# A recurrent stack on one core: step loops written out, the early layers cut into 64-step pieces, and the input projection accumulated in the gates' PSUM rows

## The chip, the cores and the metric

One core of a Trainium2 chip runs one kernel. The number that counts is the device time of one execution in microseconds (us). Five engines work side by side: TensorE (PE, matmuls; its weight loads are listed as PEld), VectorE (DVE), ScalarE (ACT), GpSimd (POOL) and SyncE (SP, which issues most DMAs). They wait for each other through semaphores. Lines such as L763 are lines of the kernel before; lines of the changed kernel are named as "line 520 after".

## The reference, cut to what matters

The input x is 2 sequences of 1024 time steps, 256 wide. Four layers are applied, each added to its input:

1. attention of every token to two keys made from a condition vector (16 heads);
2. a mixture of experts: 4 blocks of shared hidden units (`silu(x sw1) * (x sw3)`) and 8 experts of 128 units with an exact gelu, of which the best 2 per token count;
3. a linear map plus a vector made from the condition;
4. a recurrence over the 1024 steps:

```python
xz = jnp.einsum('ntd,dk->ntk', x, Wx) + b
def step(carry, xz_t):
    prev_h, prev_c = carry
    z = xz_t + prev_h @ Wh
    ai, af, ao, ag = jnp.split(z, 4, axis=1)
    i = sigmoid(ai); f = sigmoid(af); o = sigmoid(ao); g = tanh(ag)
    next_c = f * prev_c + i * g
    next_h = o * jnp.tanh(next_c)
```

Layers 1 to 3 have no dependence between tokens. Layer 4 is a chain of 1024 steps, each on 2 sequences x 256 values. All arithmetic is in float32.

## The kernel before, in words

**A step of the recurrence.** PE multiplies the last h (2 columns of weights, since there are 2 sequences) with the 1024 columns of Wh. The 64 columns that belong to one j (j = 0 to 3) go to PSUM partitions 32j and on, so four products with different j run beside each other in four column strips of the array. Three groups come out one after the other: input and forget gate together (bank 0, moving tensor of 128 columns, semaphore `z_if`), the candidate (bank 1, 64 columns, `z_c`), the output gate (bank 2, 64 columns, `z_o`). That is 24 matmuls of the program. The trace lists each float32 matmul as 2 records, so 48 at L1075. DVE transposes each group in 32x32 blocks (L763, L765, L772), so that the 256 gate values lie on 128 partitions, 4 to a partition and gate. ACT takes sigmoid, tanh and sigmoid (L507, L510, L512). DVE multiplies forget gate and old cell (L769) and makes the new cell with one scan of 8 elements (L776), ACT its tanh (L514), DVE the new h (L782), and that releases PE for the next step.

**The projected input.** x Wx + b is computed for 256 steps at a time (`gate_inputs`, L1022, L700), stored to DRAM and brought back in pieces of 4 steps to `staged`. In each step 12 further matmuls (L1065, 24 records) with columns of an identity put the step's rows into the three banks before the recurrent products are added. Each waits until its bank has been transposed (`t_if`, `t_c`, `t_o`).

**The early layers.** There are 4 chunks of 256 time steps (512 tokens). Layers 1 to 3 of chunk 0, and layer 1 and the router of all four, run ahead of the recurrence. Layers 2 and 3 of chunk m+1 run as jobs in the 256 steps of chunk m: in every step one matmul of 128x128 weights on 128 tokens (L1089), its weights copied by SP to `blocks`. At the start of a chunk SP also spreads the experts' gates over all partitions (`comb_all`, 2048 KB). After step 64 of a chunk ACT takes the exact gelu of all experts at once (L530), with a table load on either side. Between two chunks the rest of `gate_inputs` runs with no step beside it.

**Loops.** Every engine runs a device loop whose body is 8 steps, or 16 in the stage of the shared units (steps 64 to 127 of a chunk), where PE's body is twice as long.

## Time and profile before

| | |
|---|---|
| median of 3 runs | 2500.44 us (2494.17 to 2506.16) |
| span of the profiled execution (first to last instruction) | 2496.8 us |
| PE busy, share of the span | 2227.9 us, 89% |
| DVE busy | 1230.2 us, 49% |
| ACT busy | 660.5 us, 26% |
| mean granted TensorE clock | 0.973 |
| instructions fetched by DMA (queues 8 and 14) | 4.93 MB |

The only own time that the page gives for the profiled execution is its span, 2496.8 us; the median of the timed runs lies 3.6 us above it. Busy time of PE counts records that lie over each other once. A busy PE is not a PE at its peak: matmuls are pipelined, and a record of 64 columns is 0.219 us long while the next begins after a fraction of that. The idle time ahead of an instruction is printed in brackets, with what ended it; "issue" is time in which the engine waited for nothing that the trace shows.

### The profile page before, as it was taken

What the parts mean: (1) busy time and instruction counts of PE and PEld (TensorE: products, weight loads), DVE (VectorE), ACT (ScalarE), POOL (GpSimd) and SP (SyncE); (2) the same over time, 40 slices, a digit from 0 to 9 for tenths busy, and PEclk for the clock granted to TensorE, in tenths of its full rate; (3) what the DMA queues carried; (4) which work ended last, traced back from release to release, by engine and by line L of the source; (5) the groups of instructions that cost most, each with busy time, mean ns of one, the idle gap of its engine ahead of it and who ended that gap; (6) DMA issues with size and microseconds to landing.
All of it is one profiled execution on the core that took longest, in us unless ns stands there. A gap on an engine that the chain in (4) does not pass through costs nothing.

```text
span 2496.8 us, 171522 instructions
## 1 busy us (share of the span) xinstructions
PE 2227.9 (89%) x75688; PEld 1647.1 (66%) x75688; DVE 1230.2 (49%) x6361; ACT 660.5 (26%) x4183; POOL 44.5 (2%) x141
## 2 busy tenths in 40 slices
PE   8989788989989988898998988799899888888888
PEld 5477666767767766676776766677677555555555
DVE  4345454545544445454554444455455455555554
ACT  1123322222222322222222232222222222222222
POOL 0000000000000000000000000000000000000000
PEclk9999999999999999999999999899999999999999
DMA  5100000000020000000002000000000100000000
GB/s 200 57 26 11 13 14 18 13 14 12 9 80 12 11 12 15 18 12 14 12 10 80 12 11 14 13 19 13 13 11 9 43 4 4 4 8 4 4 4 7
DMA packets 41946, 53.73 MB, mean 22 GB/s; under 512 B 7584, under 2 KB 35616, under 8 KB 40608
## 3 DMA queue, kind: packets, MB, share of 16 engines
q1 hardware_dynamic: 40048, 47.23, 5.8%
q8 instruction: 288, 4.72, 0.8%
q10 hardware_dynamic: 1584, 1.57, 0.2%
q14 instruction: 26, 0.21, 0.0%
HBM read 26.83 MB, written 10.55 MB: 15 GB/s over the span
## 4 chain that ended last, share of the span: by engine, by line
PE 42%; DVE 30%; ACT 17%; issue 11%; DVEq 0%; DMA 0%; ACTq 0%; SPq 0%; POOL 0%; POOLq 0%
PE bank L1075 29%; DVE bank L763 12%; ACT if_act L507 7%; DVE bank L772 7%; ACT o_act L512 6%; DVE h_ring L782 6%; DVE if_act L769 6%; PE bank L1065 4%; ACT bank L514 4%; PE bank L1089 3%; PE bank L1022 2%; PE bank L1006 1%; PE bank L912 1%; PE bank L924 1%; ACT hidden L530 0%
## 5 line engine op out<-in xcount | busy, mean ns | idle before, releaser
L1075 PE MATMUL bank<-wh_sb,h_ring 128*2 128x128 f32 (+1 forms) x49152 | 1123.4, 239 | 125.1 <-DVE h_ring L782 56.1
L1075 PEld LDWEIGHTS bank<-wh_sb,h_ring 128*2 128x2 f32 x49152 | 906.2, 85 | 321.5 <-DVE h_ring L782 284.0
L1065 PE MATMUL bank<-staged,small_sb 128*2 128x64 f32 (+1 forms) x24576 | 707.1, 239 | 51.9 <-issue 13.2
L763 DVE STREAM_TRANSPOSE bank<-bank 128x128 f32<-128x128 f32 x1024 | 338.7, 331 | 822.0 <-PE bank L1075 821.5
L1065 PEld LDWEIGHTS bank<-staged,small_sb 128*2 128x2 f32 x24576 | 440.0, 85 | 272.3 <-DVE bank L772 76.2
L507 ACT ACTIVATE if_act<-bank 128x8 f32<-128x8 f32 x1024 | 182.2, 178 | 1485.2 <-DVE bank L763 1485.1
L782 DVE TENSOR_TENSOR h_ring<-o_act,bank 128x4 f32<-128x4 f32 x1024 | 162.0, 158 | 230.7 <-ACT bank L514 230.7
L772 DVE STREAM_TRANSPOSE bank<-bank 128x64 f32<-128x64 f32 x1024 | 263.3, 257 | 8.3 <-PE bank L1075 5.7
L765 DVE STREAM_TRANSPOSE bank<-bank 128x64 f32<-128x64 f32 x1024 | 253.1, 247 | 3.7 <-PE bank L1075 1.1
L512 ACT ACTIVATE o_act<-bank 128x4 f32<-128x4 f32 x1024 | 177.3, 173 | 275.4 <-DVE bank L772 274.3
L1089 PE MATMUL bank<-stream,blocks 128*128 x768 | 195.0, 337 | 58.1 <-issue 58.1
L769 DVE TENSOR_TENSOR if_act<-if_act,bank 128x4 f32<-128x4 f32 x1024 | 162.3, 158 | 101.6 <-ACT if_act L507 14.3
L1089 PEld LDWEIGHTS bank<-stream,blocks 128*128 128x128 f32 x768 | 119.5, 196 | 108.8 <-issue 70.4
L776 DVE TENSOR_TENSOR_SCAN bank<-bank,if_act 128x8 f32<-128x8 f32 x1024 | 184.7, 180 | 0.0
L510 ACT ACTIVATE bank<-bank 128x4 f32<-128x4 f32 x1024 | 161.8, 158 | 6.7 <-DVE bank L765 6.2
L514 ACT ACTIVATE bank<-bank 128x4 f32<-128x4 f32 x1024 | 162.2, 158 | 0.1
L1089 PE MATMUL bank<-hidden,blocks 128*128 (+1 forms) x576 | 142.4, 328 | 18.8 <-issue 18.8
L1089 PEld LDWEIGHTS bank<-hidden,blocks 128*128 128x128 f32 x576 | 86.6, 190 | 53.8 <-issue 23.3
L428 POOL TENSOR_TENSOR stream<-stream,h_ring 128x32 f32 x128 | 34.2, 267 | 2352.6 <-DVE h_ring L782 2352.6
L1022 PE MATMUL bank<-wx_sb,x 128*128 128x512 f32 x104 | 45.7, 596 | 1.0 <-DVE x L686 1.0
L1022 PEld LDWEIGHTS bank<-wx_sb,x 128*128 128x128 f32 x104 | 19.4, 190 | 25.2 <-issue 22.2
L700 DVE TENSOR_TENSOR xz_sb<-bank,bias_z_sb 128x512 f32<-128x512 f32 x26 | 18.0, 691 | 27.1 <-PE bank L1022 27.1
(99 smaller groups left out, 400.0 us busy)
## 6 DMA issues: line engine op xcount, KB each, us to landing
blocks<-moe_sb SPq DMA_DIRECT2D x170, 64.0 KB, 1.8
comb_all<-comb_scratch SPq DMA_DIRECT2D x4, 2048.0 KB, 7.8
xz_scratch<-xz_sb SPq DMA_DIRECT2D x16, 512.0 KB, 2.9
staged<-xz_scratch SPq DMA_DIRECT2D x496, 16.0 KB
moe_sb<-in_moe SPq DMA_DIRECT2D x1, 2048.0 KB, 10.3
out_y<-stream SPq DMA_DIRECT2D x8, 256.0 KB, 2.7
moe_sb<-in_moe SPq DMA_DIRECT2D x1, 1536.0 KB, 15.2
stream<-in_x ACTq DMA_DIRECT2D x3, 512.0 KB, 21.6
```

The lines of the kernel that those rows point to most:

```text
L507: nc.scalar.activation(if_act[:, par, :, :, 0], t_if_b[:, 0:2, :, 0:B], ACT.Sigmoid).then_inc(a_if, 1)
L512: nc.scalar.activation(o_act[:, par, :], t_if_b[:, 2, :, 0:B], ACT.Sigmoid).then_inc(a_o, 1)
L514: nc.scalar.activation(c_tanh[:, par, :], cell_b[:, par, :, 1], ACT.Tanh).then_inc(cell_tanh, 1)
L763: nc.vector.transpose(bank[3][:, 0:2 * HC], bank[0][:, 0:2 * HC]).then_inc(t_if, 1)
L765: nc.vector.transpose(bank[4][:, 0:HC], bank[1][:, 0:HC]).then_inc(t_c, 1)
L769: nc.vector.tensor_tensor(if_act[:, par, 0, :, 1], if_act[:, par, 1, :, 0], cell_b[:, 1 - par, :, 1], ALU.mult).then_inc(kept, 1)
L772: nc.vector.transpose(bank[3][:, 2 * HC:3 * HC], bank[2][:, 0:HC]).then_inc(t_o, 1)
L776: nc.vector.tensor_tensor_scan(cell_b[:, par, :, :].rearrange("p q k -> p (q k)"), g_pairs[:, par, :, :].rearrange("p q k -> p (q k)"), if ...
L782: nc.vector.tensor_tensor(h_ring[:, u, :, :].rearrange("p c b -> p (c b)"), o_act[:, par, :], c_tanh[:, par, :], ALU.mult).then_inc(hid, 1)
L1065: last = nc.tensor.matmul(z[32 * j:32 * j + B, 0:(g1 - g0) * HC].rearrange("p (g m) -> p g m", m=HC), ident[:, k:k + HU + 1:HU], staged_v[ ...
L1075: last = nc.tensor.matmul(z[32 * j:32 * j + B, 0:(g1 - g0) * HC].rearrange("p (g m) -> p g m", m=HC), h_ring[:, prev, c, :], wh_v[:, c, g0 ...
L1089: last = nc.tensor.matmul(bank[7][:, tile * P:(tile + 1) * P], lhs(n), rhs(n, tile), start=start and u == 0, stop=stop and n == 1, skip_gr ...
```

## The change: what it does

1. **Loops.** All 1024 steps are written out; no engine has a loop or a counted register any more.
2. **Chunks.** Layers 1 to 3 are done for 64 steps (128 tokens) at a time. Chunk 0 runs ahead of the recurrence. Chunk n+1 runs as jobs in the 64 steps of chunk n by a fixed table of step numbers: scores 0, attention 2, router 4, gates 5 to 12, units 12 to 35, down projection 37 to 48 (two matmuls a step), linear map 49 and 50. Steps 51 to 63 have no job. All weights stay in SBUF: the copies to `blocks`, the round trip of `xz_scratch`, and `comb_all` are gone. The gates of an expert are spread over the partitions by a matmul with the identity (line 642 after). Stores to the output, 18 in place of 8, are all that SP issues once the loads are out.
3. **Input in the gates' rows.** The stationary operand of a recurrent product is a window of `h_ring` with zeros ahead of the two columns of h, so that the two result rows land at row 2u of the bank, u being the step's place in a group of 8. The rows of 8 steps are filled beforehand by x Wx and the bias, in one `inject` per bank and 8 steps: 12 matmuls for the forget gate, 12 for the output gate, and 24 for the bank that holds candidate (rows 0 to 15) and input gate (rows 16 to 31). The three injections fall into different steps of the 8 (3, 5 and 7). So the stationary operand has 2 to 16 columns (18 to 32 for the input gate) in place of 2.
4. **Groups.** The order is forget gate (8 matmuls), candidate and input gate into one bank (16), output gate (8): 32 of the program a step, all with a moving tensor of 64 columns. DVE transposes three times 64 columns.
5. **Input gate through tanh.** Its weights are halved once by POOL, and sigmoid(a) = (1 + tanh(a/2))/2 is used; the factor goes into the scan, which has 12 elements in place of 8. The cell is kept doubled, and its tanh has a scale of 0.5.
6. **gelu** is computed as x(1+erf(x/sqrt 2))/2, so that ACT needs one table throughout.

```diff
-                    for z, g0, g1, made, _ in groups:
-                        for c in range(C):
-                            for j in range(J):
-                                last = nc.tensor.matmul(
-                                    z[32 * j:32 * j + B, 0:(g1 - g0) * HC].rearrange("p (g m) -> p g m", m=HC),
-                                    h_ring[:, prev, c, :], wh_v[:, c, g0:g1, j, :],
-                                    start=False, stop=(c == C - 1), skip_group_check=True)
-                        last.then_inc(made, 1)
...
+            def recur(z, g, row, prev):
+                for c in range(C):
+                    for j in range(J):
+                        last = nc.tensor.matmul(z[32 * j:32 * j + row + B, 0:HC],
+                                                h_ring[:, prev, c, WIN - B - row:WIN], wh_v[:, c, g, j, :],
+                                                start=False, stop=(c == C - 1), skip_group_check=True)
+                return last
...
+            def inject(z, g, columns, bias_of, rows, start):
...
+                for c in range(C):
+                    for j in range(J):
+                        nc.tensor.matmul(z[32 * j:32 * j + rows, 0:HC], columns(c), wx_v[:, c, g, j, :],
+                                         start=(start and c == 0), stop=False, skip_group_check=True)
+                for j in range(J):
+                    nc.tensor.matmul(z[32 * j:32 * j + rows, 0:HC], bias_of, bias_v[:, g, j, :],
+                                     start=False, stop=False, skip_group_check=True)
...
+            def step(t):
+                uf, ug, uo, prev = (t + 4) % U, t % U, (t + 2) % U, (t - 1) % U
+                pe.wait_ge(hid, t + 1)
+                recur(z_f_b, GF, uf * B, prev).then_inc(z_f, 1)
+                recur(z_gi_b, GC, ug * B, prev)
+                recur(z_gi_b, GI, 16 + ug * B, prev).then_inc(z_gi, 1)
+                recur(z_o_b, GO, uo * B, prev).then_inc(z_o, 1)
+                if uf == U - 1:
+                    inject_stream(z_f_b, GF, t, t_f)
+                if ug == U - 1:
+                    inject_gi(t)
+                if uo == U - 1:
+                    inject_stream(z_o_b, GO, t, t_o)
...
+            for t in range(T):
+                step(t)
+                if t // TC + 1 < CHUNKS:
+                    side(t // TC + 1, t % TC)
```

The two injections that wait for a transpose late in the step are the one at step 7 of 8 (`inject_gi` waits for `t_gi`) and the one at step 5 of 8 (it waits for `t_o`). A job of the same step stands behind them on PE.

What PE does in a step before, in program order (L1065: input rows; L1075: recurrent products; L1089: job; the shape is the matmul's output, partitions x columns):

```order
L1075 MATMUL bank<-wh_sb,h_ring 2x128 x8
L1075 MATMUL bank<-wh_sb,h_ring 2x64 x16
L1089 ISA
L1089 MATMUL bank<-stream,blocks 128x128
L1063 REGISTER_ALU
L1065 MATMUL bank<-staged,small_sb 2x128 x4
L1065 MATMUL bank<-staged,small_sb 2x64 x8
```

What PE does after, where step 7 of 8 ends and the next step begins (lines 593 and on of that kernel: L691 recurrent products, L700 and L703 injection, L642 and L627 jobs):

```order
L691 MATMUL bank<-wh_sb,h_ring 4x64 x8
L700 MATMUL bank<-wx_sb,padded 32x64 x8
L703 MATMUL bank<-bias_sb,small_sb 32x64 x4
L700 MATMUL bank<-wx_sb,padded 16x64 x8
L703 MATMUL bank<-bias_sb,small_sb 16x64 x4
L642 MATMUL bank<-small_sb,comb 128x128
L691 MATMUL bank<-wh_sb,h_ring 10x64 x8
L691 MATMUL bank<-wh_sb,h_ring 2x64 x8
L691 MATMUL bank<-wh_sb,h_ring 18x64 x8
L691 MATMUL bank<-wh_sb,h_ring 6x64 x8
L627 MATMUL bank<-stream,moe_sb 128x128 x2
```

The input rows have left seven steps of eight, and where they stand they are 24 matmuls in a block, with a job between them and the next step's first product.

DVE before, one step (L763 and L765 transpose, L769 product, L772 transpose, L776 scan, L782 new h):

```order
L763 STREAM_TRANSPOSE bank<-bank 128x128
L765 STREAM_TRANSPOSE bank<-bank 128x64
L769 TENSOR_TENSOR if_act<-if_act,bank 128x4
L772 STREAM_TRANSPOSE bank<-bank 128x64
L776 SCALAR_TENSOR_TENSOR bank<-bank,if_act 128x8
L782 TENSOR_TENSOR h_ring<-o_act,bank 128x4
```

DVE after, one step with a job (L520 transposes the forget gate, L522 candidate and input gate, L527 the output gate; L530 is the scan; L486 is layer 2's addition):

```order
L520 STREAM_TRANSPOSE bank<-bank 128x64
L522 STREAM_TRANSPOSE bank<-bank 128x64
L525 TENSOR_TENSOR terms<-f_act,bank 128x4
L527 STREAM_TRANSPOSE bank<-bank 128x64
L530 SCALAR_TENSOR_TENSOR bank<-terms 128x12
L532 TENSOR_TENSOR h_ring<-o_act,bank 128x2x2
L486 SCALAR_TENSOR_TENSOR stream<-bank,stream 128x2x128
```

The number of operations is the same. The first transpose is half as wide, the second now stands for two gates, the scan is longer, and jobs come behind the new h.

## Rows read from the trace of the kernel before

**Rows 1.** Timeline, one step, last chunk: start us, us, engine, line, op, [idle before].

```profile
2300.44 1.06 PE L1075 MATMUL bank<-wh_sb,h_ring 128*2 128x128 f32 x48 [0.20 <-DVE h_ring L782]
2301.13 0.33 DVE L763 STREAM_TRANSPOSE bank<-bank 128x128 f32<-128x128 f32 x1 [0.74 <-PE bank L1075]
2301.37 0.25 DVE L765 STREAM_TRANSPOSE bank<-bank 128x64 f32<-128x64 f32 x1
2301.49 0.18 ACT L507 ACTIVATE if_act<-bank 128x8 f32<-128x8 f32 x1 [1.30 <-DVE bank L763]
...
2301.70 0.16 DVE L769 TENSOR_TENSOR if_act<-if_act,bank 128x4 f32<-128x4 f32 x1
2301.78 0.26 DVE L772 STREAM_TRANSPOSE bank<-bank 128x64 f32<-128x64 f32 x1
2301.97 0.18 DVE L776 TENSOR_TENSOR_SCAN bank<-bank,if_act 128x8 f32<-128x8 f32 x1
...
2302.18 0.16 ACT L514 ACTIVATE bank<-bank 128x4 f32<-128x4 f32 x1
2302.37 0.16 DVE L782 TENSOR_TENSOR h_ring<-o_act,bank 128x4 f32<-128x4 f32 x1 [0.22 <-ACT bank L514]
...
2302.59 1.06 PE L1075 MATMUL bank<-wh_sb,h_ring 128*2 128x128 f32 x48 [0.20 <-DVE h_ring L782]
```

**Rows 2.** Windows, L782 alone: window, length, DVE busy (steps), clock, DMA share, GB/s.

```profile
119.00:716.00 597.00, 40.48 (x256) 0.97 0.06 17
716.00:731.50 15.50, 0.16 (x1) 0.89 0.48 177
...
1935.00:1947.00 12.00, 0.16 (x1) 1.00 0.53 200
1947.00:2494.00 547.00, 40.34 (x255) 1.00 0.02 4
```

**Rows 3.** Timeline: three kinds of stall, first chunk.

```profile
130.20 0.29 PE L1075 MATMUL bank<-wh_sb,h_ring 128*2 128x64 f32 x6 [2.91 <-issue]
...
261.57 3.62 ACT L530 ACTIVATE hidden<-hidden 128x4096 f32<-128x4096 f32 x1
...
266.50 0.18 ACT L507 ACTIVATE if_act<-bank 128x8 f32<-128x8 f32 x1
...
305.96 0.50 PEld L1089 LDWEIGHTS bank<-stream,blocks 128*128 128x128 f32 x2 [5.18 <-issue]
...
309.73 0.33 DVE L763 STREAM_TRANSPOSE bank<-bank 128x128 f32<-128x128 f32 x1 [7.65 <-PE bank L1075]
```

**Rows 4.** Windows, front: PE, PEld, DVE, ACT, POOL busy, clock, DMA share, GB/s.

```profile
0.00:30.00 30.00, 22.77 (x94) 15.76 (x95) 6.62 (x21) 2.33 (x4) 3.04 (x6) 0.86 0.92 344
```

**Rows 5.** Timeline, front: first and last operation of one gate computation.

```profile
28.34 0.19 DVE L628 TENSOR_TENSOR sel<-s_all,small_sb 128x32 f32<-128x32 f32 x1 [0.29 <-ACT s_all L465]
...
32.34 0.19 DVE L652 TENSOR_TENSOR comb<-comb_a,comb_b 128x32 f32<-128x32 f32 x1
```

**Rows 6.** Timeline: one 128x128 job, and sixteen projections of 512 columns.

```profile
1200.79 0.49 PE L1089 MATMUL bank<-hidden,blocks 128*128 x2
...
102.64 14.00 PE L1022 MATMUL bank<-wx_sb,x 128*128 128x512 f32 x32 [1.04 <-DVE x L686]
```

**Rows 7.** Timeline, front: runs of weight loads, 16 and 128 columns wide.

```profile
11.38 0.29 PEld L865 LDWEIGHTS bank<-small_sb,k_heads 128*16 128x16 f32 x8
...
18.53 0.97 PEld L942 LDWEIGHTS bank<-small_sb,wproj_sb 128*128 128x128 f32 x8 [0.42 <-issue]
```

**Rows 8.** Timeline, the recurrent products of a step after a stall.

```profile
1009.36 1.93 PE L1075 MATMUL bank<-wh_sb,h_ring 128*2 128x128 f32 x48
```

**Rows 9.** Windows, that stretch and the last chunk (columns of Rows 4).

```profile
1001.00:1011.20 10.20, 7.14 (x148) 5.48 (x148) 1.73 (x9) 0.75 (x5) 0.00 (x0) 0.50 0.02 4
1950.00:2450.00 500.00, 433.67 (x16792) 292.61 (x16792) 254.47 (x1402) 136.26 (x935) 7.79 (x29) 1.00 0.02 4
```

**Rows 10.** Timeline, the last DMA issue.

```profile
2493.78 0.61 SPq L352 DMA_DIRECT2D out_y<-stream  x1
```

More of the change, by code:

```diff
@@ L845, in _ @@
+            layer2(0)
+            layer3(0)
+            dve.wait_ge(cleared, 5)
+            for t in range(T):
+                step(t)
+                if t // TC + 1 < CHUNKS:
+                    side(t // TC + 1, t % TC)
         @block.tensor
         def _(pe):
+            pe.wait_ge(cell, 1)
             pe.wait_ge(small_in, 16)
@@ L867, in _, with scores @@
             last.then_inc(score_made, 1)
-            def scores(i):
-                pe.wait_ge(x_in[i], 16)
-                if i > 0:
-                    pe.wait_ge(w1_out, i * B)
-                for b in range(B):
+            def scores(n):
+                pe.wait_ge(x_in[x_part(n)], 16)
+                for c in range(C):
+                    last = nc.tensor.matmul(bank[6][0:B * HEADS, 0:NT], score_w[:, c, :], stream[:, c, tokens(n)],
+                                            start=(c == 0), stop=(c == C - 1))
+                last.then_inc(scores_made, 1)
@@ new lines, in up @@
+            def up(n, j):
+                if j == 0:
+                    pe.wait_ge(s_out, n + 1)
+                elif j >= 2:
+                    pe.wait_ge(unit_out, n * UNITS + j - 1)
+                at = 4 * j if j < MS else EXPERT_AT + 2 * (j - MS)
+                for c in range(C):
+                    last = nc.tensor.matmul(bank[UP_BANK[j % 2]][:, 0:NT], moe_sb[:, at + c, :],
+                                            stream[:, c, tokens(n)], start=(c == 0), stop=(c == C - 1))
+                last.then_inc(up_made, 1)
@@ L875, in scores, with up2 @@
+            def up2(n, j):
+                out = bank[UP_BANK[j % 2]][:, NT:2 * NT]
+                pe.wait_ge(act_out, n * UNITS + j + 1)
+                if j < MS:
                     for c in range(C):
[L876 to L877 removed]
+                        last = nc.tensor.matmul(out, moe_sb[:, 4 * j + 2 + c, :], stream[:, c, tokens(n)],
@@ new lines, in up2, with down @@
+                last.then_inc(up2_made, 1)
+            def down(n, i):
+                for k2 in range(2):
+                    c, k = divmod(2 * i + k2, UNITS)
+                    if c == 0:
+                        pe.wait_ge(unit_out, n * UNITS + max(k + 1, UNITS - 1))
+                    last = nc.tensor.matmul(bank[6][:, c * NT:(c + 1) * NT], moe_sb[:, DOWN_AT + c * UNITS + k, :],
+                                            hidden[:, k, :], start=(k == 0), stop=(k == UNITS - 1))
+                if i == UNITS - 1:
+                    last.then_inc(down_made, 1)
@@ new lines, in lin @@
+            def lin(n, c):
+                pe.wait_ge(x2_out, n + 1)
+                out = bank[7][:, c * NT:(c + 1) * NT]
+                for k in range(C):
+                    nc.tensor.matmul(out, we_sb[:, k, c * P:(c + 1) * P], stream[:, k, tokens(n)],
+                                     start=(k == 0), stop=False)
+                last = nc.tensor.matmul(out, cond_out[:, c * P:(c + 1) * P], pick, start=False, stop=True)
+                if c == C - 1:
+                    last.then_inc(lin_made, 1)
@@ L1164, in _ @@
-            with pe.Fori(0, CITERS) as k:
-                steps(k + (CHUNKS - 1) * CITERS)
+            pe.wait_ge(w_in["experts"], 16)
+            for j in range(MS, UNITS):
+                up(0, j)
+                up2(0, j)
+                if j == MS + 2:
+                    pe.wait_ge(w_in["wu"], 16)
+                    pe.wait_ge(u_out, 1)
+                    for m in range(C):
+                        last = nc.tensor.matmul(bank[0][0:B, D:2 * D], u_act[:, m, :], wu_sb[:, m, :],
+                                                start=(m == 0), stop=(m == C - 1))
+                    last.then_inc(cond_made, 1)
@@ new lines, in _ @@
+            pe.wait_ge(w_in["down"], 16)
+            for i in range(UNITS):
+                down(0, i)
+            pe.wait_ge(w_in["we"], 16)
+            pe.wait_ge(cond_done, 1)
+            for c in range(C):
+                lin(0, c)
+            pe.wait_ge(halved, 2)
+            inject_stream(z_f_b, GF, -5, None)
+            inject_stream(z_o_b, GO, -3, None)
+            inject_gi(-1)
+            pe.wait_ge(halved, 3)
+            for t in range(T):
+                step(t)
+                if t // TC + 1 < CHUNKS:
+                    side(t // TC + 1, t % TC)
```

1189 lines of the change are left out of this document (431 added, 758 removed).

## The prediction, as it was put on record

> **What bounds the kernel now.** I read the timeline of one undisturbed step first, then counted steps per stretch, then looked at the stalls and at the front.
>
> The timeline [rows 1] shows a chain that never has slack. PE starts the recurrent products at 2300.44. DVE's first transpose starts 0.69 later, ACT's sigmoid at 1.05, DVE's product at 1.26, the scan at 1.53, ACT's tanh of the cell at 1.74, the new h at 1.93, and PE starts again at 2.15. Two bounds meet at the scan. Along the first gates it could not start before the product (0.16) is done at 1.42; what holds it to 1.53 is the output gate's transpose, which starts 0.08 behind the product and lets the next DVE instruction go after 0.19.
>
> The windows that hold only the instruction of the new h [rows 2] give the rest. In the last chunk 255 steps take 547 us, 2.145 each (I use 2.144; PE's two starts in the timeline are 2.15 apart). The first chunk has 256 steps in 597 us, 48 more than 256 x 2.144 = 549; the next two chunks are alike. Between two chunks stand 15.5 (twice) and 12.0 us with a single step. So the three chunks lose 3 x 48 = 144 us inside and about 37 between, 180 together. Check, with the first products at 117.67 and the last new h at 2493.16 [rows 10]: 117.7 + 1.9 + 1023 x 2.144 (2193.3) + 180 + 3.6 of tail = 2496.5, against a span of 2496.8.
>
> The stalls [rows 3] are of three kinds. PE waits for nothing visible ("issue"): 5.18 us at 305.96, where the long loop body begins again, with DVE idle for 7.65; two more like it follow in each chunk. ACT holds up a step with the gelu of 4096 elements (3.62) and a table load on either side. And PE stands for 2.91 within the first pass through a body at 130, while 2048 KB of expert gates are spread.
>
> **The change, part by part.**
>
> *Loops, gelu batch, spreading, stage between chunks.* All that made the 180 us is gone: no branch, one ACT table, no `comb_all`, no stage without steps. Minus 180, if the written-out code arrives in time (a rival below).
>
> *Front, now 117.7 us.* Chunk 0 is 128 tokens in place of 512, and only its part of layer 1 runs ahead. The start up to the score weights stays, 11.8 us. I put layer 1 of one chunk at 6 more, the gates at 3.5 (the 14 operations take 4.2 for four times the elements, and most of that is fixed [rows 5]), 12 units at 1.4 (two jobs of 0.49 [rows 6], 0.3 of ACT and hand-overs, one behind the other), 24 down products at 0.21 to 0.43 depending on the clock, and 4 for the linear map, the padding and the injections. That is 11.8+6+3.5+16.8+8+4 = 50. The 7.9 MB up to Wh need 23 us at the 344 GB/s of the first 30 [rows 4], so they don't bind. Bounds 43 and 65. Minus 68.
>
> *A step, now 2.144.* The 48 records span 1.06, a record of 64 columns takes 0.219, and counted in units of 64 columns there are 16 rounds of four strips: (1.06-0.22)/15 = 0.056 a round. The first gates' last round begins 6 units in, 0.34; with 0.27 for a record of 128 columns that leaves 0.08 until DVE starts at 0.69 [rows 1]. After the change there are again 16 rounds: forget gate 4, candidate and input gate 8, output gate 4. So DVE can start the forget gate at 3x0.056+0.22+0.08 = 0.47, candidate+input at 11x0.056+0.30 = 0.92, the output gate at 15x0.056+0.30 = 1.14. From there, by [rows 1]: transpose 0.25, hand-over 0.03, tanh of 8 elements 0.18, hand-over 0.03, so the scan may start at 1.41. On DVE the product follows the second transpose by 0.19 (1.11), the third transpose by 0.08 (1.19), the scan by 0.19 (1.38), so now the tanh holds it, at 1.41. The scan to the cell's tanh takes 0.21 and 0.02 for four more elements, then 0.19 and 0.22: next start at 2.05. Gain 0.09 a step. The forget gate is ready at 0.93, 0.18 ahead of need; if DVE is late with it, nothing moves up to there. Halving the weights costs nothing in the steps. POOL's sum (0.3 us a group of 8) lies under PE's 0.47. All steps: 50 + 1.8 + 1023 x 2.05 (2097) + 3.6 = 2153.
>
> *Injections and jobs.* The 12 program matmuls a step leave, 48 a group of 8 steps come. They start when the bank has been transposed: for candidate+input at 1.17+0.06 = 1.23, 12 rounds of 0.056 to 1.90, for the output gate at 1.50, 6 rounds to 1.84; the forget gate's ends at 1.25. Alone each fits before 2.05. A job behind it does not: a 128x128 matmul streams 0.21 (14.0 us for 32 records of 512 columns, 0.44 each, so 0.11 a record of 128, two a matmul [rows 6]). Two matmuls after `inject_gi` end at 2.33, 0.28 late, in steps 15, 39 and 47 of a chunk; one ends 0.06 late in 23 and 31; after the output gate's, two are 0.22 late in 13, 37 and 45. Sum 3x0.28+2x0.06+3x0.22 = 1.6 a chunk, 24 us for 15 chunks. What waits behind them is the whole next step. If each change between full-array and strip products costs 0.2 more in the ten exposed places, it is 30 us more. I take 30. DVE's and ACT's jobs have at most 256 and 128 columns and lie in the 0.5 us in which DVE waits for PE; the waits on jobs of the same step are met there except in those steps. 2183.
>
> *Wider stationary operands.* No row shows strips with more than 2 columns. Runs of full loads [rows 7] show 128 columns every (0.97-0.19)/7 = 0.111 us, 0.87 ns a column. If the four strips load at the same time, 32 columns take 0.03, under a round. If they load one after another, a round of R columns needs 3.5R ns: more than 0.056 above 16 columns, that is for the input gate alone (18 to 32, mean 25: 0.087). Four rounds x 0.031 = 0.12 a step. I take the first, since with 2 columns the strips' records begin side by side, and keep 0.12 x 1023 = 127 us as the upper end. By the Trainium skill, TensorEngine Tiling (Array Packing), Key Properties, different tiles can execute their weight loads and matmuls in parallel; by that the sum would get no such term. The trace before neither confirms nor denies it for wide loads.
>
> *The clock.* It is at 1.00 (2.4 GHz) throughout the last chunk [rows 9], where PE streams 16 rounds and 8 more of input rows in 2.144: 63%. It is at 0.50 (1.2 GHz) in 1001 to 1011, after PE had stood through a stall. After the change five steps of eight without a job stream 16 rounds, 0.90 of 2.05: 44%; no stretch of before lies that low without a stall. A step at half clock: 48 records span 1.93 [rows 8], a round 0.112; the output gate then arrives at 15x0.112+0.30 = 1.98, the scan starts at 2.17, the step takes 2.81, 0.76 more. I allow some 30 such steps, 20 us (bounds 0 and 100). 2203.
>
> **Sum.** 50 + 2 + 2097 + 30 + 20 + 4 = 2203 of span, and 3.6 as the median lies over the span before: 2207 us.
>
> **The rivals.**
>
> *Serial weight loads.* As above: 2207+127 = 2334. For it: a column costs time in every run of loads. Against it: the strips' products stream beside each other. 20%.
>
> *Half clock for long stretches (the other side).* If the granted clock falls in steps without a job or injection and stays down, each step costs 0.76 more. With all steps at half: 50+1023x2.81+30 = 2960. It decides from (2500-2190)/0.76 = 410 steps at half, 40%: below that the kernel is still faster. For it: 44% streaming in place of 63%. Against it: jobs and injections fill PE to 70% and more in half the steps. The Trainium skill, TensorE: Matmul & The Clock Gate, Part 1, says that the gate's state is set by how busy PE has been recently; by that rule this change is at risk, and the trace agrees that the clock falls only after PE has idled. 7% that it costs more than the gain, 8% that it costs 100 to 300 us (2300 to 2490).
>
> *Code comes too late.* PE has 38 to 40 program matmuls a step to fetch, 37 before. Stalls of 5 us at every return to the 16-step body, if they came every 16 steps, would cost 64 x 5 = 320: 2527, slower. Against it: after each such stall the body's steps run on without an issue stall, and the one at 130 fell together with 2 MB of other traffic, which is gone. 4%.
>
> **Chances.** Forecast 61%, serial loads 20%, long half clock 8% and 7%, code 4%. The likeliest case alone spans 2150 to 2260 (front 43 to 65, step 2.03 to 2.07, jobs 24 to 60, clock 0 to 60). The range 2150 to 2350 takes in serial loads and leaves out less than 2 in 10. A measurement of this kernel can tell 0.5%, 12 us, from nothing. Faster 90% (all but the two slower cases), within 0.5% 1%, slower 9%.
>
> **What would show it.** First transposes to first transposes 2.05 in steps 51 to 63 of a chunk, with L520 starting 0.47 and L522 0.92 after PE. If L522 drifts from 0.92 to 1.1 as the rows go from 18 to 32, loads are serial; if L527 starts later than 1.2, PE is slower than I count. Steps of 2.3 at 15, 39, 47. The clock row of those stretches: anything under 1.00 there means the 20 us are too few. The first h after 52 us. Idle "issue" of PE should be near nothing. The prediction is wrong if a step's period is over 2.1 at full clock, or if the clock is below 0.9.

## The result, and the profile after

The changed kernel takes 2527.55 us (median of 4 runs, 2523.85 to 2537.98) against 2500.91 of the kernel before beside it: a ratio of 1.011, 95% interval 1.009 to 1.014. It is 1.1% slower; 2207 was forecast, and the rival with the nearest mechanism, "code comes too late", had 4%.

The page of the changed kernel (busy time, clock by slices, instruction queue, the chain that ended last):

```profile
span 2536.1 us, 173932 instructions
...
PE 1946.1 (77%) x80392; PEld 1551.4 (61%) x80392; DVE 1275.4 (50%) x6871; ACT 738.7 (29%) x4322; POOL 44.1 (2%) x154
...
PEclk9999999999899999999999999999999999989999
...
q8 instruction: 630, 10.32, 1.7%
...
PE 59%; DVE 23%; issue 10%; ACT 7%; DVEq 0%; DMA 0%; SPq 0%; POOLq 0%; POOL 0%
```

PE is busy for 282 us less than before and the time is still longer. The instruction queue moves 630 pages of 16 KB, where the kernel before moved 288 (4.72 of its 4.93 MB); queue 8 carries PE's instructions, as the kernel with PE in a loop shows below. The share of "issue" in the chain, 10%, tells nothing by itself: it was 11% before. The mean granted clock is 0.956. This execution is the slowest of the four, 10 us above their median.

The timeline of a step whose chain nothing disturbs, to set beside [rows 1] (L520, L522, L527 transposes, L340 the tanh of candidate and input gate, L530 the scan, L532 the new h):

```profile
1196.55 1.08 PE L691 MATMUL bank<-wh_sb,h_ring 128*6 128x64 f32 x64
...
1197.03 0.27 DVE L520 STREAM_TRANSPOSE bank<-bank 128x64 f32<-128x64 f32 x1
...
1197.48 0.27 DVE L522 STREAM_TRANSPOSE bank<-bank 128x64 f32<-128x64 f32 x1 [0.18 <-PE bank L691]
...
1197.65 0.15 DVE L525 TENSOR_TENSOR terms<-f_act,bank 128x4 f32<-128x4 f32 x1
1197.70 0.27 DVE L527 STREAM_TRANSPOSE bank<-bank 128x64 f32<-128x64 f32 x1
1197.78 0.18 ACT L340 ACTIVATE terms<-bank 128x8 f32<-128x8 f32 x1 [0.27 <-DVE bank L522]
...
1198.06 0.19 DVE L530 TENSOR_TENSOR_SCAN bank<-terms 128x12 f32<-128x12 f32 x1
...
1198.47 0.16 DVE L532 TENSOR_TENSOR h_ring<-o_act,bank 128x4 f32<-128x4 f32 x1 [0.22 <-ACT bank L346]
...
1198.68 0.21 PEld L691 LDWEIGHTS bank<-wh_sb,h_ring 128*8 128x8 f32 x13 [0.60 <-DVE h_ring L532]
```

The transposes start 0.48 and 0.93 after PE, as forecast (0.47, 0.92). The scan starts at 1.51, not 1.41: the tanh is done at 1197.96 and the scan begins 0.10 later. The step is 2.13 long.

Two steps further on (same timeline, PE), an injection with a job behind it, and the next step:

```profile
1200.48 0.43 PE L700 MATMUL bank<-wx_sb,padded 128*32 128x64 f32 x16 [0.23 <-DVE bank L522]
...
1200.84 0.31 PE L703 MATMUL bank<-bias_sb,small_sb 1*32 1x64 f32 x8
...
1201.09 0.42 PE L700 MATMUL bank<-wx_sb,padded 128*16 128x64 f32 x16
...
1201.43 0.30 PE L703 MATMUL bank<-bias_sb,small_sb 1*16 1x64 f32 x8
...
1201.66 0.49 PE L642 MATMUL bank<-small_sb,comb 128*128 128x128 f32 x2
...
1202.08 0.56 PE L691 MATMUL bank<-wh_sb,h_ring 128*10 128x64 f32 x25
...
1203.30 0.74 PE L691 MATMUL bank<-wh_sb,h_ring 128*2 128x64 f32 x39 [0.66 <-issue]
```

The injection takes 1.18 to the job's start in place of the 0.67 of 12 rounds; the bias matmuls, which contract over 1 row and not 128, start late behind their neighbours (tried below). And in the middle of the recurrent products, whose operands are all there, PE stands for 0.66 with nothing to wait for. The view of waits sums the idle time of this kind (us, times, longest):

```profile
PEld bank L700 <- issue: 137.9, 275, 0.8
...
PEld bank L691 <- issue: 78.3, 154, 2.0
...
PE bank L691 <- issue: 48.7, 97, 1.8
```

The two lines of L691 are the interrupted recurrent products. The line of L700 is not such a place: it comes about once an injection, and in the kernel "pair alone" below, in which no recurrent burst is interrupted, the same place still has 146.3 us in 257 times. The breaks are tied to the pages of code. In the trace, 127 times a record inside a recurrent burst starts more than 0.25 us behind the one before; 122 of these breaks end 2.2 to 2.9 us after a page's transfer on queue 8 began, a stretch into which 17% of all recurrent records fall. Between 1000 and 1500 us (the DMA view of that window) 127 pages come, one per 3.94 us:

```profile
q8 instruction: 127, 2.08, 1.7%
```

**Where the 333 us between the sum (2203) and the span (2536.1) are.** I took the starts of L532, and for each of the 64 places in a chunk the shortest step among chunks 1 to 14; this "undisturbed chunk" is 145.0 us. Ten places without job or injection in it have a median of 2.133; such a step is called quiet below, and "excess" is what steps take beyond the undisturbed chunk.

| term | forecast | measured | difference |
|---|---|---|---|
| first new h | 52 | 61.4 | +9 |
| 1023 steps | 2.05 each | 2.133 each | +85 |
| injections and jobs: (145.0 - 64 x 2.133) x 15 | 30 | 127 | +97 |
| what goes beyond the undisturbed chunk | 20 (clock) | 163 | +143 |

The last row is 79 us in some 800 steps of chunks 1 to 14 at full clock, 58 in some 95 steps that touch a stretch at half clock, and 25 in the first and last chunk.

The sum of before rested on two times that [rows 10] was to show and does not; in the timeline of the kernel before they are:

```profile
117.67 0.60 PE L1075 MATMUL bank<-wh_sb,h_ring 128*2 128x128 f32 x13 [0.26 <-DVE h_ring L749]
```

```profile
2493.16 0.16 DVE L782 TENSOR_TENSOR h_ring<-o_act,bank 128x4 f32<-128x4 f32 x1 [0.23 <-ACT bank L514]
```

### The profile page after: what moved, and what is told of

The parts are those of the page before. It is cut to its first block, busy times and chain, and to the rows that moved or that the text cites. A ratio compares the mean times of both kernels' runs of the same rounds, so it can differ in the third digit from the quotient of the medians.

```text
span 2536.1 us, 173932 instructions
## 1 busy us (share of the span) xinstructions
PE 1946.1 (77%) x80392; PEld 1551.4 (61%) x80392; DVE 1275.4 (50%) x6871; ACT 738.7 (29%) x4322; POOL 44.1 (2%) x154
## 4 chain that ended last, share of the span: by engine, by line
PE 59%; DVE 23%; issue 10%; ACT 7%; DVEq 0%; DMA 0%; SPq 0%; POOLq 0%; POOL 0%
PE bank L691 41%; DVE bank L522 9%; PE bank L700 7%; DVE bank L530 5%; DVE h_ring L532 5%; ACT bank L346 4%; PE bank L703 4%; DVE bank L527 4%; PE bank L651 2%; ACT terms L340 2%; PE bank L637 1%; PE bank L642 1%; DVE terms L525 1%; PE bank L660 1%; PE bank L627 1%
## 5 line engine op out<-in xcount | busy, mean ns | idle before, releaser
L691 PE MATMUL bank<-wh_sb,h_ring 128*10 128x64 f32 (+3 forms) x65536 | 1213.3, 226 | 472.0 <-DVE h_ring L532 418.6
L691 PEld LDWEIGHTS bank<-wh_sb,h_ring 128*10 128x10 f32 (+3 forms) x65536 | 995.5, 97 | 674.1 <-DVE h_ring L532 559.6
L520 DVE STREAM_TRANSPOSE bank<-bank 128x64 f32<-128x64 f32 x1024 | 271.9, 265 | 515.0 <-PE bank L691 507.4
L337 ACT ACTIVATE f_act<-bank 128x4 f32<-128x4 f32 x1024 | 177.9, 174 | 1200.5 <-DVE bank L520 1200.5
L522 DVE STREAM_TRANSPOSE bank<-bank 128x64 f32<-128x64 f32 x1024 | 271.8, 265 | 258.9 <-PE bank L691 248.6
L527 DVE STREAM_TRANSPOSE bank<-bank 128x64 f32<-128x64 f32 x1024 | 271.7, 265 | 37.4 <-PE bank L691 30.2
L340 ACT ACTIVATE terms<-bank 128x8 f32<-128x8 f32 x1024 | 185.5, 181 | 352.8 <-DVE bank L522 352.8
L532 DVE TENSOR_TENSOR h_ring<-o_act,bank 128x4 f32<-128x4 f32 x1024 | 163.2, 159 | 231.1 <-ACT bank L346 231.1
L530 DVE TENSOR_TENSOR_SCAN bank<-terms 128x12 f32<-128x12 f32 x1024 | 192.4, 188 | 84.1 <-ACT terms L340 2.2
L346 ACT ACTIVATE bank<-bank 128x4 f32<-128x4 f32 x1024 | 162.4, 159 | 99.9 <-DVE bank L530 2.3
L703 PE MATMUL bank<-bias_sb,small_sb 1*16 1x64 f32 (+1 forms) x4112 | 164.6, 226 | 3.7 <-issue 3.3
L700 PE MATMUL bank<-wx_sb,stream 128*16 128x64 f32 x4128 | 115.2, 227 | 65.0 <-DVE bank L527 60.9
L525 DVE TENSOR_TENSOR terms<-f_act,bank 128x4 f32<-128x4 f32 x1024 | 152.4, 149 | 0.2
L627 PE MATMUL bank<-stream,moe_sb 128*128 128x128 f32 x768 | 141.2, 306 | 3.4 <-issue 2.9
L700 PE MATMUL bank<-wx_sb,padded 128*32 128x64 f32 (+1 forms) x4096 | 113.2, 226 | 29.7 <-DVE bank L522 29.0
L700 PEld LDWEIGHTS bank<-wx_sb,stream 128*16 128x16 f32 x4128 | 75.2, 99 | 87.0 <-issue 86.7
L627 PEld LDWEIGHTS bank<-stream,moe_sb 128*128 128x128 f32 x768 | 104.1, 196 | 24.9 <-issue 4.8
L700 PEld LDWEIGHTS bank<-wx_sb,padded 128*32 128x32 f32 (+1 forms) x4096 | 71.8, 104 | 63.4 <-issue 51.2
L703 PEld LDWEIGHTS bank<-bias_sb,small_sb 1*16 1x16 f32 (+1 forms) x4112 | 71.0, 93 | 61.4 <-issue 12.6
```

The costliest lines, as they stand in the source:

```text
L340: nc.scalar.activation(gi_out.rearrange("p g (c b) -> p g c b", b=B), t_gi_b[:, :, :, ug * B:(ug + 1) * B], ACT.Tanh).then_inc(a_gi, 1)
L346: nc.scalar.activation(c_tanh, cell_c, ACT.Tanh, scale=0.5).then_inc(cell_tanh, 1)
L520: nc.vector.transpose(bank[3][:, 0:HC], z_f_b[:, 0:HC]).then_inc(t_f, 1)
L522: nc.vector.transpose(bank[4][:, 0:HC], z_gi_b[:, 0:HC]).then_inc(t_gi, 1)
L527: nc.vector.transpose(bank[3][:, HC:2 * HC], z_o_b[:, 0:HC]).then_inc(t_o, 1)
L530: nc.vector.tensor_tensor_scan(cell_all, factor, addend, 0.0, ALU.mult, ALU.add).then_inc(cell, 1)
```

## The experiments

Every kernel ran beside the kernel before on the same chip; the ratios are to that. The groups of runs used different chips; the kernel before took 2498 to 2504 us beside them.

### One mended cost at a time

Two waits stand on the scan; the one for the tanh came last.

```diff
-                dve.wait_ge(kept, t + 1)
                 dve.wait_ge(a_gi, t + 1)
+                dve.wait_ge(kept, t + 1)
```

> The changed kernel with one pair of lines exchanged: the scan waits for the tanh of candidate and input gate first and for its own product second. In the trace of the changed kernel the wait for the tanh is an instruction of its own on VectorE, and the scan starts 0.065 us behind it, where before that wait stood on the scan itself and the hand-over took 0.033. Theory A (the order of the two waits costs a hand-over): a clean step falls from 2.137 to about 2.07 us, 1023 x 0.065 = 67 us less where VectorE is the bound, some 55 in all: about 2470. Rival B (the scan is held by the third transpose, or by TensorE): no change, 2527. Rival C (TensorE's code arrives no faster than one 16 KB piece in some 3.4 us, 157 instructions a step being 0.61 of a piece, 2.09 us a step): half of the gain is given back as idle time of the kind issue, about 2500.

The bias rows, 1 partition in place of 128 (the other 127 are zeros):

```diff
-        bias_sb = sb("bias_sb", [1, G4])
+        bias_sb = sb("bias_sb", [P, G4])
...
-        ones = part("ones")[0:1, :]
+        ones = part("ones")
```

> The changed kernel with the bias held on 128 partitions (127 of them zero), so that the bias matmuls of the injections contract over 128 rows like their neighbours and no longer over one. Theory A (each change of the number of rows empties the array, 0.11 to 0.14 us each, four of them in the injection for candidate and input gate): the step behind that injection falls from 2.52 to about 2.2 us, with a job behind it from 3.16 to about 2.85, the steps with job behind the output gate's injection by 0.13; 2.8 us a chunk, about 45 in all: about 2483. Rival B (the gaps are waits for code or for the weight loads): same gaps, 2527.

The job ahead of the injections that wait for a late transpose:

```diff
                 recur(z_o_b, GO, uo * B, prev).then_inc(z_o, 1)
+                if job and ahead:
+                    side(t // TC + 1, t % TC)
                 if uf == U - 1:
...
+                if job and not ahead:
+                    side(t // TC + 1, t % TC)
```

> The changed kernel with TensorE's job of a step placed ahead of the injection in the steps where the injection waits for a late transpose (steps 5 and 7 of each 8). The same instructions in another order. Theory A (the job's 0.43 plus a change of tiling of 0.2 fit into TensorE's wait for the transpose): the ten steps of a chunk that now take 2.55 to 3.16 us fall by 0.3 to 0.6 each, 4 to 5 us a chunk, 60 to 75 in all: about 2460. Rival B (TensorE has no slack there: the job only pushes the injection back by as much): within 10 us of 2527.

One extra matmul of 256 columns in steps with neither job nor injection:

```diff
+                if quiet and U - 1 not in (uf, ug, uo):
+                    pe.wait_ge(s_out, min(t // TC + 2, CHUNKS))
+                    nc.tensor.matmul(bank[6][:, 256:512], moe_sb[:, 0, :], wh_sb[:, 0, 0:256],
+                                     start=True, stop=True)
```

> The changed kernel with one extra matmul of 128x128 weights on 256 columns, whose result nobody reads, behind the recurrent products of each step that has neither job nor injection. Four more instructions in such a step. Theory A (the granted clock falls in the quiet stretches because TensorE streams too little there): clock near 1.00 in steps 52 to 63 of each chunk and in the last chunk, mean clock over 0.98, steps there 2.14 throughout, 50 to 70 us less: about 2465. Rival B (the clock falls because TensorE stands still waiting for code): mean clock stays at 0.956, time 2527 or up to 10 us more.

| run | us | ratio, 95% | undisturbed chunk | excess at full clock | mean clock |
|---|---|---|---|---|---|
| changed kernel | 2527.55 | 1.011 (1.009 to 1.014) | 145.0 | 79 | 0.956 |
| scan's wait | 2494.98 | 0.998 (0.996 to 1.001) | 141.3 | 101 | 0.956 |
| bias on 128 rows | 2495.64 | 0.999 (0.997 to 1.002) | 141.2 | 118 | 0.965 |
| job first | 2494.46 | 0.998 (0.996 to 1.000) | 140.9 | 107 | 0.955 |
| filler | 2492.58 | 0.997 (0.995 to 1.000) | 144.8 | 103 | 0.993 |

The undisturbed chunk or the clock shows that each cost was real. With the waits exchanged the scan follows the tanh by 0.03 (timeline of that kernel):

```profile
1201.04 0.18 ACT L340 ACTIVATE terms<-bank 128x8 f32<-128x8 f32 x1 [0.27 <-DVE bank L522]
1201.25 0.19 DVE L530 TENSOR_TENSOR_SCAN bank<-terms 128x12 f32<-128x12 f32 x1
```

and the quiet step is 2.071. With 128 rows an injection's bias starts 0.22 to 0.23 behind the x rows, not 0.34 to 0.36 (timeline of PE, the same place in the group of 8):

```profile
1199.91 0.43 PE L700 MATMUL bank<-wx_sb,padded 128*32 128x64 f32 x16 [0.25 <-DVE bank L522]
1200.13 0.32 PE L703 MATMUL bank<-bias_sb,small_sb 128*32 128x64 f32 x8
1200.24 0.43 PE L700 MATMUL bank<-wx_sb,padded 128*16 128x64 f32 x16
1200.47 0.32 PE L703 MATMUL bank<-bias_sb,small_sb 128*16 128x64 f32 x8
1200.72 0.49 PE L642 MATMUL bank<-small_sb,comb 128*128 128x128 f32 x2
```

To the job's start it is 0.81, not 1.18. But all four arrive within 3 us of each other, although the undisturbed chunks promise 56 to 62 us (3.7 to 4.1 x 15) for three of them, and a clock of 0.993 about 50 for the fourth. In each the excess at full clock rises, by 22 to 39 us. That is what something else that holds the rate would do.

### Is it the code? The same instructions from a loop

> The scan's wait for the tanh alone, the bias on 128 rows and the jobs ahead of the injections, all three. Without losses their undisturbed chunks add up: 3.7 + 3.8 + 4.1 = 11.6 us shorter than the 145.0 of the changed kernel, 174 us for 15 chunks. Theory 'code arrives too slowly' (a page of 16 KB, 256 PE records' worth of instructions, cannot come more often than about every 3.4 us, and 630 pages are needed): the excess over the undisturbed chunk grows again, by 60 to 100 us, and the time is 2400 to 2450. Rival 'the three overlap in the same steps and nothing is given back': the undisturbed chunk itself falls by less than 8 us and the excess stays at 135. Second rival 'nothing is lost': 2527 - 174 = 2353.

The next two leave work out, as their expectation says. PE's instructions are the same in both but for the loop and its registers:

```diff
-            for t in range(T):
-                step(t % U, t + 1)
+            with pe.Fori(0, T // U) as it:
+                count = [pe.snap(it * U + u + 1) for u in range(U)]
+                for u in range(U):
+                    step(u, count[u])
```

> Leaves out: layers 1 to 3 of all chunks but the first, every injection takes the first eight rows of chunk 0, and an erf is a tanh. Has the scan's wait and the 128-row bias of the runs before, and one extra matmul of 256 columns in every step without an injection, so that the clock stays up. All 1024 steps written out. About 157 PE instructions a step. Theory 'code arrives too slowly': at a step of 2.07 us a page is needed every 3.4 us, at the rate at which they come, so issue stalls inside the recurrent products go on although there is no job: 30 or more over 0.2 us, mean step above 2.07 at full clock, steps 2150 to 2350 in all, about 600 pages on queue 8. Rivals 'the stalls belong to the jobs, to contention between job and recurrence' : no issue stalls here, steps within 20 us of those of the next run.

> As the run before, the same instructions in the same order, but PE's stand in a device loop of eight steps (counted waits against registers); the other engines stay written out. Theory 'code arrives too slowly': the body stays loaded, queue 8 moves fewer than 60 pages, the issue stalls inside the products vanish and the step is 2.07 to 2.10 throughout: steps 2120 to 2160 in all, plus what is left of half clock, and 50 to 200 us less than written out. Rival 'the stalls come with such products or with the clock, not with their fetching': as many issue stalls as written out, the same time within 20 us, or more for the branch.

And code that costs PE hardly any time, added to the first of this group:

```diff
+                    for k in range(8):
+                        j = k % J
+                        nc.tensor.matmul(bank[6][32 * j:32 * j + B, 256:257], h_ring[:, prev, 0, WIN - B:WIN],
+                                         wh_v[:, 0, GF, j, 0:1], start=True, stop=True, skip_group_check=True)
```

> The three changes together, and eight more strip matmuls of one column (32 instructions) in each of some 220 steps that have neither a job nor an injection, right behind the output gate's products, where PE then idles for over 0.8 us. They add about 7,000 instructions, 27 pages. Theory 'code arrives too slowly': such a step needs 170 instructions, a page every 1.5 steps, and can't be shorter than 170/256 of 3.4 = 2.27; the time rises by 40 to 90 us over the three together, with more issue stalls. Rival 'PE's time in these steps is free': no change, within 10 us.

"Pages" are those of queue 8 in the whole run, "1023 steps" the us from the first new h to the last, and "us a page" is the one over the other.

| run | us | ratio, 95% | pages | 1023 steps | us a page | excess at full clock |
|---|---|---|---|---|---|---|
| three together | 2486.93 | 0.994 (0.992 to 0.996) | 630 | 2415 | 3.83 | 208 |
| no jobs, written out | 2370.22 | 0.946 (0.944 to 0.948) | 620 | 2313 | 3.73 | 171 |
| no jobs, PE in a loop | 2191.42 | 0.876 (0.873 to 0.878) | 7 | 2130 | | 4 |
| ballast | 2579.38 | 1.028 (1.024 to 1.032) | 655 | 2512 | 3.84 | 239 |

The waits of the two kernels without jobs, first written out, then with PE in a loop:

```profile
PEld bank L687 <- issue: 175.9, 229, 1.7
PE bank L687 <- issue: 134.6, 212, 1.5
```

```profile
PEld bank L687 <- issue: 2.0, 2, 1.7
PE bank L687 <- issue: 1.7, 2, 1.5
```

and the windows of the new h alone over the same 500 us (columns of [rows 2]), in the same order:

```profile
1000.00:1500.00 500.00, 35.20 (x221) 1.00 0.02 5
```

```profile
1000.00:1500.00 500.00, 38.23 (x240) 1.00 0.00 1
```

The clock is 1.00 in both, the chain of a step is the same (undisturbed chunks 132.3 and 132.9), and 179 us go with the fetching. This decides against jobs, contention and the clock as the cause of the stalls. No page starts less than 3.2 us behind the one before in any of the written-out kernels.

The ballast points the same way, with a part left open: PE's new matmuls stand where it idles, and the time rises by 92 us for 25 pages. That this is 3.7 us a page is in part chance, since the clock fell too, from a mean of 0.965 to 0.946. Of the 97 us by which the 1023 steps of the two profiled executions differ, 57 lie in the 834 steps that ran at full clock in both, and 40 in the rest; whether the clock fell because PE stood longer for code is not shown. The three mended costs together shorten the undisturbed chunk by 11.6 us, 174 in 15 chunks, of which 41 arrive; the excess at full clock takes 129 of the rest (79 to 208).

### Fewer instructions

If the code sets the rate, the same arithmetic in fewer instructions is worth more than a shorter chain. Candidate and input gate go side by side in columns of their bank, as the kernel before had input and forget gate: 24 matmuls a step in place of 32, at the price of a transpose of 128 columns.

```diff
-                recur(z_gi_b, GC, ug * B, prev)
-                recur(z_gi_b, GI, 16 + ug * B, prev).then_inc(z_gi, 1)
+                recur(z_gi_b, PAIR, ug * B, prev).then_inc(z_gi, 1)
...
-                nc.vector.transpose(bank[4][:, 0:HC], z_gi_b[:, 0:HC]).then_inc(t_gi, 1)
+                nc.vector.transpose(bank[4][:, 0:2 * HC], z_gi_b[:, 0:2 * HC]).then_inc(t_gi, 1)
```

> The three changes together, and candidate and input gate side by side in 128 columns of their bank in place of 16 rows each: 24 matmuls a step in place of 32, 36 in the injections of 8 steps in place of 48, the same streaming of 16 rounds of 64 columns. One fewer form of work for POOL. 9,728 fewer matmuls of the program, 152 pages: 478 in place of 630, a page every 4.4 us. DVE's second transpose gets 128 columns, 0.07 longer on the chain, as the first transpose of the kernel before (0.33 against 0.25). Theory 'code arrives too slowly': issue stalls inside the products nearly vanish, the step is 2.07 + 0.07 = 2.14, in all 56 + 1023 x 2.14 (2189) + 15 for steps with jobs + 50 half clock + 4 = 2314 (2280 to 2350). Rival 'not the fetching': the time rises by the longer transpose, 2487 + 72 = 2559.

> As the run before, with one extra matmul of 256 columns in every step that has neither job nor injection, which keeps the clock up (0.993 with it on the changed kernel, against 0.956). There it gave back in issue stalls half of what it won. Theory 'code arrives too slowly': now there is room for its instructions (4 in a step of some 115), so what is left of the half clock, some 50 us, is won whole: 2265 (2240 to 2300). Rival 'the clock's loss is made up elsewhere': within 10 us of the run before.

> The changed kernel with candidate and input gate in columns and nothing else: its hand-over from tanh to scan, its one-row bias and its order of jobs stay. Theory 'code arrives too slowly': the step is 0.07 longer (2.21), the steps with injections keep their extra (some 90 us), but the issue stalls inside the products go: 61 + 1023 x 2.21 (2261) + 90 + 60 half clock + 4 = 2476 (2440 to 2510), faster than the changed kernel in spite of the longer transpose. Rival 'not the fetching': 2527 + 72 - 20 (fewer bias matmuls) = 2579.

> Candidate and input gate in columns, and the scan's wait for the tanh alone; the one-row bias and the order of the jobs stay. It asks why the run with the columns alone still had 263 us at half clock (mean 0.947), and the one with all four edits 9 (0.998). Theory 'the clock follows how densely the quiet steps use PE': with the hand-over mended they are 2.12 long in place of 2.19, as in the run with all four, and the clock stays above 0.98: 57 + 15 x 143 + 134 + 4 = 2340 (2320 to 2365). Rival 'the clock falls behind the one-row bias matmuls and the changes of mode around them': the clock stays at 0.95, and the time is 60 higher, 2400. In both the step has the same code, 478 pages, and no issue stalls in the recurrent products.

| run | us | ratio, 95% | undisturbed chunk | quiet step | excess at full clock | half clock, us | mean clock |
|---|---|---|---|---|---|---|---|
| pair, with the three | 2249.69 | 0.901 (0.899 to 0.903) | 136.3 | 2.119 | 4 | 9 | 0.998 |
| the same with filler | 2244.07 | 0.898 (0.896 to 0.900) | 136.3 | 2.119 | 3 | 9 | 0.998 |
| pair alone | 2478.47 | 0.991 (0.988 to 0.993) | 146.4 | 2.187 | 4 | 263 | 0.947 |
| pair and scan's wait | 2384.78 | 0.951 (0.949 to 0.954) | 143.0 | 2.124 | 4 | 176 | 0.964 |

They move 478 pages (481 with the filler), and in all four the excess at full clock is gone; in "pair, with the three" and "pair alone" no record inside a recurrent burst is more than 0.25 us late. The pair alone is 49 us faster than the changed kernel although its quiet step is 0.054 longer. With the three mended costs, which were worth 41 us together before, it is 229 us faster still: 151 is the shorter undisturbed chunk (146.4 to 136.3, 15 times), which now arrives, and some 60 is the excess of the steps that touched half clock, which is gone too. That kernel takes 10% less than the kernel before. Its page and one of its steps (L505, L507, L512 transposes, L325 the tanh, L515 the scan, L517 the new h):

```profile
q8 instruction: 478, 7.83, 1.5%
...
PE 55%; DVE 26%; ACT 12%; issue 7%; DMA 0%; SPq 0%; POOLq 0%; POOL 0%; DVEq 0%
```

```profile
1197.69 1.07 PE L681 MATMUL bank<-wh_sb,h_ring 128*8 128x64 f32 x48 [0.41 <-DVE h_ring L517]
1198.17 0.27 DVE L505 STREAM_TRANSPOSE bank<-bank 128x64 f32<-128x64 f32 x1 [0.34 <-PE bank L681]
...
1198.60 0.33 DVE L507 STREAM_TRANSPOSE bank<-bank 128x128 f32<-128x128 f32 x1 [0.17 <-PE bank L681]
...
1198.97 0.18 ACT L325 ACTIVATE terms<-bank 128x8 f32<-128x8 f32 x1 [0.33 <-DVE bank L507]
...
1199.18 0.19 DVE L515 TENSOR_TENSOR_SCAN bank<-terms 128x12 f32<-128x12 f32 x1
...
1199.60 0.16 DVE L517 TENSOR_TENSOR h_ring<-o_act,bank 128x4 f32<-128x4 f32 x1 [0.22 <-ACT bank L331]
...
1199.81 0.89 PEld L681 LDWEIGHTS bank<-wh_sb,h_ring 128*10 128x10 f32 x48
```

The step is 2.12 from start to start, though a job and an injection lie in it on PE. I had expected 2314 and 2265 for the first two. Both came out lower: the quiet step is 2.119 and not 2.14, 21 us in 1023 steps, and in the first the 50 us put down for half clock did not come, since the clock stayed up without the filler (the filler's 6 us are less than these runs tell apart).

Why the clock stays up is only half settled. The windows of the last chunk without jobs, of the pair with the three, the pair with the scan's wait, and the pair alone (columns of [rows 4]: PE, PEld, DVE, ACT, POOL busy, clock, DMA share, GB/s):

```profile
2105.00:2238.00 133.00, 79.55 (x3576) 65.93 (x3564) 71.92 (x376) 42.78 (x250) 1.85 (x8) 1.00 0.02 6
```

```profile
2258.00:2390.00 132.00, 84.25 (x3388) 66.00 (x3392) 67.88 (x355) 39.88 (x236) 1.77 (x7) 0.94 0.02 4
```

```profile
2324.00:2470.00 146.00, 92.95 (x3514) 71.76 (x3508) 71.65 (x371) 42.11 (x248) 1.76 (x7) 0.88 0.02 5
```

The first two have the same step outside the injections and the same matmuls; they differ in the bias on 128 rows or on 1 (no job is left to be moved there), and the clock is 1.00 or 0.94. Against the second, the third has the longer step, and 0.88. As the clocks stand, both expected answers of the last run are partly right: it is higher with the shorter step, and higher again with the bias on 128 rows. But the first and the third ran on one chip, the second on another; that the chip has a share in its 0.94 is not excluded, and each window is of one execution.

## Why the prediction was wrong

**The step that failed.** "Minus 180, if the written-out code arrives in time (a rival below)". It doesn't. The rival had the right name and the wrong mechanism: I priced a stall of 5 us at every return to a long body, 320 in all. That its 2527 is the measured time is luck: the excess at full clock is 79 us, and other terms make up the rest. What the runs show is a rate: straight code comes at one page of 16 KB, about 256 PE records (2 x 80392 records in 630 pages), per 3.7 to 3.9 us. The 38 program matmuls of a step are 152 records, with the jobs 157 on average (2 x 80392 in 1024 steps), so 157/256 x 3.73 = 2.29 us: the code of an average step takes longer to fetch than the forecast step of 2.05. 1023 of them need 2340, and at that rate no shortening of the chain gets below it. My argument against it, that after a stall the body's steps run on, came from loop bodies already fetched.

This step alone does not account for the miss. With fewer instructions and the other costs left in, the time is 2478; with the three costs mended and the instructions left in, 2487; only both together give 2250, inside the range. Two terms of the sum were mis-sized by as much as the code: the step (85 us) and the injections with their jobs (97 us). My own sign of being wrong, a period over 2.1 at full clock, came true with 2.133.

The trace of before held the number. In its DMA view of 262 to 465 us, where PE's loop bodies are longer than 8 steps, and in the windows of the new h there and in the two stretches behind it:

```profile
q8 instruction: 52, 0.85, 1.8%
```

```profile
262.00:465.00 203.00, 12.34 (x78) 0.92 0.06 15
520.00:574.00 54.00, 3.48 (x22) 0.94 0.05 14
576.00:628.00 52.00, 3.95 (x25) 1.00 0.04 12
```

52 pages in 203 us are 3.9 each, and 78 steps take 2.60 each; in 520 to 574, where 15 pages come, a step takes 2.45, in 576 to 628, with no page at all, 2.14. Pages at nearly that rate need not cost: in the 16 steps from 544 us, 9 come in 34.5 us, and a step takes 2.15. I had given the 48 us that a chunk loses inside [rows 2] to single stalls [rows 3]; that a large part of them was this rate is argued from these windows, not tried, and half clock has a share in them too (0.92 and 0.94).

**Point by point.**

- *Loops, gelu, spreading, stage between chunks, -180.* Those stalls are gone, and others came: 79 us of excess at full clock, which fall to 4 once PE has 24% fewer instructions. The fetching costs more than it shows, as it swallows what else is mended (174 us promised, 41 received).
- *Front, 50.* First new h at 61.4 against 52. In the runs with jobs and 32 matmuls a step it came between 55.4 and 67.9, so 52 was too early by at least 3 us, and the rest is within what it varies by.
- *A step, 2.05.* The first two transposes start as forecast to 0.01; the third at 1.15, where I had put 1.19, which moves nothing, since the scan waits for the tanh. The term "hand-over 0.03" between tanh and scan was the error: 0.10, because the wait for the tanh was the second of two on the scan. Exchanged, the quiet step is 2.071; the 0.02 left are in the transposes, 0.27 in place of 0.25. Mis-sized by 85 us in all.
- *Injections and jobs, 30.* "If each change between full-array and strip products costs 0.2 more in the ten exposed places" counted the job's borders and not those of the bias, which contracts over one row: 0.11 to 0.14 at each of the three inside an `inject_gi` (1.18 against 0.81 in all); the job's own borders cost the same with either bias. It is 127 us. Two matmuls behind `inject_gi` make the next step 3.16 and not 2.3, and steps that I had counted as free (the injections without a job) were late too, 2.52 behind `inject_gi`. The 30 was small by its own working: 24 for late jobs and 30 for the borders are 54. Moving the bias to 128 rows takes 57 us of it, jobs ahead of the injection 62.
- *Wider stationary operands.* Parallel, as taken. In the medians over the eight places of a group, whose input gate has 18 to 32 columns of weights, the second transpose starts 0.920 to 0.931 behind PE and does not rise with the columns. By the Trainium skill, TensorEngine Tiling (Array Packing), Key Properties, different tiles can execute their weight loads in parallel; here the trace agrees with its 0.920 to 0.931.
- *The clock, 20 (bounds 0 to 100).* 0.956 mean, 58 us in the steps that touch half clock. Within the bounds, three times the value taken. The long half clock of the rivals did not come: the clock is at half for 227 of 2536 us.

## What to carry to other kernels

Before writing a loop out, divide the records that PE executes in the time you hope for by what arrives: here 256 records a page, a page per 3.7 to 3.9 us, and a body of eight steps (about 1,240 records) stays loaded in a loop and costs no fetching (7 pages in the whole run, the last at 70 us). If the quotient is near one, count instructions before microseconds; matmuls with twice the moving columns halve the records at the same streaming. And where several repairs of real costs each bring the same small gain while "issue" waits inside bursts grow, look for one shared limit. The clean test of it is the same instructions from a loop; adding instructions that cost nothing else is a second one, with an eye on the clock.

## What was not expected of the hardware

- Straight code for PE arrives at a page of 16 KB per 3.7 to 3.9 us, 4 GB/s, while the DMA engines are 2% busy. In a loop of eight steps 7 pages are moved in the whole run.
- Of two waits on one DVE instruction the order matters: 0.10 from the tanh to the scan with the tanh's wait last, 0.03 with it first, 62 ns in every step's chain.
- A matmul that contracts over 1 row among others over 128 costs 0.11 to 0.14 us at each border, and with it the granted clock of otherwise equal steps was 0.94 rather than 1.00, on another chip.
- PE's mean clock was 0.992 to 0.998 in five executions without any filler, once the stalls, the long hand-over and the one-row products were all gone (0.947 to 0.949 with the stalls alone gone).
